# Adding three message parts in PSUM: 24 matmuls of 48 columns a batch in place of 8 of 144

## What is computed

```python
m = relu(node_feat[src] + edge_feat)
neigh = segment_sum(m, dst, num_segments=N)            # layer 1: one sum over edges
x = segment_sum(w[:, None] * x[c], r, num_segments=n)  # layer 2: this line twice
agg = segment_sum(x[src], dst, num_segments=n)         # layer 3: twice, with weights between
agg = segment_sum(adj_vals[:, None] * xw[edge_src], edge_dst, num_segments=N)  # layer 4
```

## Time and profile before

| | us |
|---|---|
| median of 3 runs (lowest, highest) | 10436.51 (10404.52, 10447.85) |
| the profiled execution | 10414.08 |
| its span | 10412.4 |
| six sum stages, from the first gather's record to the next pass's work | about 510 to 530 each |

### The profile page before, as it was taken

How to read it: one execution, slowest core, us unless ns; L and a number is a source line. 1 busy time by engine, 2 the same in 40 slices (tenths; PEclk the granted TensorE clock), 3 DMA queues, 4 the chain that set the end, 5 groups by cost and what they waited for, 6 DMA issues and landing times.

```text
span 10412.4 us, 220272 instructions
## 1 busy us (share of the span) xinstructions
PE 6955.9 (67%) x59989; PEld 5588.1 (54%) x59990; DVE 6952.4 (67%) x15309; ACT 3898.3 (37%) x9751; POOL 4440.2 (43%) x4277
## 2 busy tenths in 40 slices
PE   9999999997045557555675667456765576555676
PEld 9766666665034445444554455345554455555555
DVE  6544444443488887777667766777757776799874
ACT  0455555554167850066005610264016600344200
POOL 0477777777077227400770057102740076000373
PEclk9855555555555557577766766677667776555565
DMA  8233333333879877688776877688768878255675
GB/s 327 64 88 87 88 89 89 86 87 110 267 226 249 264 252 223 143 289 294 226 200 235 290 241 213 176 295 268 220 148 293 292 221 197 102 195 195 201 220 117
DMA packets 1037429, 2048.13 MB, mean 197 GB/s; under 512 B 354974, under 2 KB 476318, under 8 KB 1036958
## 3 DMA queue, kind: packets, MB, share of 16 engines
q1 hardware_dynamic: 764830, 1267.16, 37.8%
q0 software_dynamic: 242832, 700.42, 25.5%
q10 hardware_dynamic: 29680, 79.57, 2.0%
HBM read 1263.63 MB, written 783.00 MB: 197 GB/s over the span
## 4 chain that ended last, share of the span: by engine, by line
DMA 23%; POOL 21%; PE 18%; issue 17%; DVE 16%; DVEq 3%; ACT 1%; POOLq 0%; SPq 0%; ACTq 0%
POOL edge_rows L446 15%; DMA WORK<-messages_in_parts,source 13%; PE psum L778 6%; DVE WORK L1055 6%; POOL WORK L479 6%; PE psum L797 5%; DMA BIG<-edge_rows 5%; DMA WORK<-parts_by_slot 4%; PE psum L664 3%; DVE WORK L1093 2%; DVE BIG L1086 2%; ACT WORK L585 1%; DVEq L67 1%; PE psum L733 1%; PE psum L783 1%
## 5 line engine op out<-in xcount | busy, mean ns | idle before, releaser
L479 POOL DMA_INDIRECT WORK<-messages_in_parts,source x2220 | 2280.4, 1027 | 4544.1 <-DMA messages_in_parts<-WORK 3763.7
L797 PE MATMUL psum<-WORK 128*128 128x144 bf16 x17760 | 2219.8, 297 | 960.4 <-DMA WORK<-messages_in_parts,source 628.4
L797 PEld LDWEIGHTS psum<-WORK 128*128 128x128 bf16 x17760 | 1806.6, 158 | 1373.0 <-issue 674.8
L446 POOL DMA_INDIRECT edge_rows<-WORK x1664 | 1709.6, 1027 | 862.5 <-issue 857.9
L778 PE MATMUL psum<-BIG,WORK 128*128 x11840 | 1287.8, 277 | 1038.2 <-DVE WORK L1055 601.3
L585 ACT CAST WORK<-psum 128x432 bf16<-128x432 f32 x2960 | 1382.5, 522 | 1415.2 <-PE psum L778 1355.6
L862 DVE TENSOR_TENSOR WORK<-lane_k,slot_part 128x1024 bf16<-128x1024 bf16 x2220 | 1529.6, 690 | 481.9 <-PE psum L797 344.3
L1055 DVE TENSOR_SCALAR WORK<-WORK,here 128x1024 bf16<-128x1024 uint8 x2220 | 1667.8, 751 | 98.4 <-DMA WORK<-parts_by_slot 78.9
L778 PEld LDWEIGHTS psum<-BIG,WORK 128*128 128x128 bf16 x11840 | 1013.5, 121 | 1312.6 <-issue 1308.9
L783 PE MATMUL psum<-BIG,WORK 128*128 x17760 | 957.9, 215 | 839.6 <-DVE WORK L1055 732.9
L783 PEld LDWEIGHTS psum<-BIG,WORK 128*128 128x128 bf16 x17760 | 834.9, 116 | 962.7 <-issue 928.9
(11 more groups left out here) (175 smaller groups left out, 7326.7 us busy)
## 6 DMA issues: line engine op xcount, KB each, us to landing
messages_in_parts<-WORK SPq DMA_DIRECT2D x2220, 288.0 KB
WORK<-parts_by_slot SPq DMA_DIRECT2D x444, 640.0 KB, 4.9
BIG<-edge_rows SPq DMA_DIRECT2D x148, 1040.0 KB
WORK<-blocks_by_edge SPq DMA_DIRECT2D x416, 256.0 KB, 3.5
edge_rows<-BIG ACTq DMA_DIRECT2D x1, 76960.0 KB, 209.9
WORK<-in_edge_attr_dram SPq DMA_DIRECT2D x415, 96.0 KB, 2.2
WORK<-messages_in_parts,source POOLq DMA_INDIRECT x2220, 4.1
edge_rows<-WORK POOLq DMA_INDIRECT x1664
```

The lines of the kernel that those rows point to most:

```text
L446: pool.indirect_dma_start(rows_dram, bass.IndirectOffsetOnAxis(ap=at_stage[g][:, j:j + 1], axis=0), row_buf[g][:, j, :], None).then_inc(s_ ...
L479: pool.indirect_dma_start(msg[c].rearrange("p k f -> p (k f)"), None, unit_dram, bass.IndirectOffsetOnAxis(ap=source[d][:, t:t + 1], axis= ...
L797: m = pe.matmul(sum_bank(c), onehot[c % GB][:, :, k], msg[c][:, k, :], start=k == 0, stop=k == K - 1)
```

## The change

In the sum stage PE writes 48 columns for a batch instead of 144: for each k three matmuls with the same weights and one third of the message each, all 24 accumulated into the same columns. A batch has a PSUM bank of its own (five banks in turn), PE waits for `sums_added` of the batch five before instead of for the reduce of a pair, and DVE adds the 48 PSUM columns straight to the aggregate. `reduce_pair`, `pair_sum` and the semaphore `pair_sums_reduced` are gone.

```diff
@@ -204,7 +204,6 @@
         SEL = [carve(128, [T * K], BF16) for _ in range(GB)]
         part_row = [carve(128, [GB, T * K], U8) for _ in range(2)]
         msg = [carve(128, [K, W3], BF16) for _ in range(RING)]
-        pair_sum = [carve(P, [2, D]) for _ in range(GB)]
         select = [s.rearrange("p (k u) -> p k u", k=K) for s in SEL]
         onehot = [s.rearrange("p (m k) -> p m k", k=K) for s in SEL]
         z = [H[:, j * K * D:(j + 1) * K * D].rearrange("p (k f) -> p k f", f=D) for j in range(GB)]
@@ -251,8 +250,7 @@
                                            sem("degrees_summed"))
         s_store = [sem(f"messages_stored{c}") for c in range(RING)]
         s_gath = [sem(f"messages_gathered{c}") for c in range(RING)]
-        s_oh, s_sum, s_reduced, s_added = (sem("onehots_ready"), sem("batches_summed"), sem("pair_sums_reduced"),
-                                           sem("sums_added"))
+        s_oh, s_sum, s_added = sem("onehots_ready"), sem("batches_summed"), sem("sums_added")
         s_var, s_std = sem("variance_ready"), sem("deviation_ready")
         s_ones, s_node, s_tr, s_trc = (sem("bias_rows_ready"), sem("aggregate_ready"), sem("blocks_transposed"),
                                        sem("transposes_copied"))
@@ -277,7 +275,7 @@
 
         def sum_bank(c):
 
-            return bank[c // 2][:, c % 2 * W3:(c % 2 + 1) * W3]
+            return bank[c % GB][:, 0:D]
 
         def spread_bank(c, k):
 
@@ -791,10 +789,11 @@
                         n = i * RING + (c + q * BATCHES)
                         pe.wait_ge(s_gath[c], i * 16 + (q * PAIRS + 1) * 16)
                         pe.wait_ge(s_oh, n + 1)
-                        if c % 2 == 0:
-                            wait_past(pe, s_reduced, i * GB + (c // 2 + q * (BATCHES // 2) - (GB - 1)))
+                        wait_past(pe, s_added, n - (GB - 1))
                         for k in range(K):
-                            m = pe.matmul(sum_bank(c), onehot[c % GB][:, :, k], msg[c][:, k, :], start=k == 0, stop=k == K - 1)
+                            for f in range(3):
+                                m = pe.matmul(sum_bank(c), onehot[c % GB][:, :, k], msg[c][:, k, f * D:(f + 1) * D],
+                                              start=k == 0 and f == 0, stop=k == K - 1 and f == 2)
                         m.then_inc(s_sum, 1)
 
                 rounds(pe, PAIRS, sum_batches)
@@ -1110,21 +1109,13 @@
                             stage(PAIRS - 1, c)
                 dve.wait_ge(s_spread, (q + 1) * BATCHES)
 
-                def reduce_pair(i, c):
-
-                    m = i * GB + (c // 2 + q * (BATCHES // 2))
-                    dve.wait_ge(s_sum, i * RING + (c + 2 + q * BATCHES))
-                    wait_past(dve, s_added, i * RING + (c + 2 - RING + q * BATCHES))
-                    v.tensor_reduce(pair_sum[c // 2], bank[c // 2][:, 0:2 * W3]
-                                    .rearrange("p (a c f) -> p a f c", a=2, c=3), AX.X, ALU.add).then_inc(s_reduced, 1)
-
                 def add_sum(i, c, b):
 
                     n = i * RING + (c + q * BATCHES)
-                    dve.wait_ge(s_reduced, i * GB + (c // 2 + q * (BATCHES // 2) + 1))
+                    dve.wait_ge(s_sum, n + 1)
                     wait_past(dve, s_added, n)
                     o = AGG[:, ds(b * D, D)]
-                    v.tensor_tensor(o, o, pair_sum[c // 2][:, c % 2, :], ALU.add).then_inc(s_added, 1)
+                    v.tensor_tensor(o, o, sum_bank(c), ALU.add).then_inc(s_added, 1)
 
                 def collect(i):
 
@@ -1139,16 +1130,11 @@
                             add_sum(i, c - LAG, its_block[c])
                         elif not isinstance(i, int):
                             add_sum(i - 1, RING + c - LAG, its_block[c])
-                        if c % 2 == 1 and c > 1:
-                            reduce_pair(i, c - 3)
-                        elif c % 2 == 1 and not isinstance(i, int):
-                            reduce_pair(i - 1, RING - 2)
 
                 if q == 0:
                     dve.wait_ge(s_mcopied, 1)
                 rounds(dve, PAIRS, collect)
                 last = load_blocks(dve, batch_regs[0:LAG], batch_block[d][0:1, BATCHES - LAG:BATCHES])
-                reduce_pair(PAIRS - 1, RING - 2)
                 for k in range(LAG):
                     add_sum(PAIRS - 1, RING - LAG + k, last[k])
                 dve.wait_ge(s_added, (q + 1) * BATCHES)
```

## The result

| | before | changed |
|---|---|---|
| median (lowest, highest), us | 10420.51 (10403.05, 10447.85), 4 runs | 10534.44 (10514.31, 10561.96), 4 runs |
| the profiled execution, us | 10414.08 | 10514.31 |
| its span, us | 10412.4 | 10512.6 |

The ratio is 1.0109, with a 95% interval of 1.0069 to 1.0149: 1.1% slower, 114 us by the medians. The direction and the mechanism are those of the forecast; the forecast size, 268 us, was more than double.

What follows compares the result with a forecast made beforehand. POOL bounds the sum stages' first part at 1.344 us a batch; 24 loads of 64 ns make PE the bound at 1.536: +46 us a stage, +278 for six, less 10, so 10,705 us, range 10,470 to 10,910.

Steps and rivals of the forecast that it cites:

- POOL bounds the first four fifths, and DVE's saving is worth nothing: Sum stage, first part: POOL's gather and idle set 1.344 us a batch; DVE's 0.23 us reduce is saved without gain.
- The price is a strided weight load, three times as many: Sum-stage matmuls on PE: each loads weights 8 elements apart, 24 loads a batch instead of 8, 1.536 us a batch.
- The load's size, between 54 and 64 ns, taken as 64: Strided weight load on PE: bracketed from two groups of eight matmuls; at 64 ns, 24 make 1.536 us a batch.
- PE stays the bound: Last part of a sum stage: gathers need 1.68 us but run about 15 us ahead and fall back only 10 us.
- The ends of the stages, 10 us: From last reduce to next pass's work: 1.90 us falls to about 0.3, giving 1.6 us a pass, 10 in all.
- Half and full clock give the same: Sum-stage matmuls on PE: 1.536 us a batch at either clock level, since 48 columns need 40 ns even at 1.2 GHz.
- A: Sum-stage loads: strided loads are cheap when nothing separates them, POOL still bounds, 10,427 us, no change; chance 0.09.
- B: Sum-stage gathers on POOL get shorter, from 1.039 to 0.96 us, as compares come evenly: 10,284 us; chance 0.07.
- C: PE's stream of matmuls breaks at every batch, paying one load's 64 ns again, 1.60 us a batch: 10,847 us; chance 0.12.
- D: Half clock makes closely following strided loads dearer, 100 ns each, 2.4 us a batch: 12,620 us; chance 0.03.
- DVE's looser order: DVE's wait in the sum stage: adds run four batches behind, so PE has four compares ahead; counted as zero.
- The estimate of 59 ns: Strided weight load as four chunks of 32 columns at 1.84 ns a column: 59 ns, a sum of 10,440 us.

Runs made afterwards that it cites:

- the DVE part alone: Changed kernel with 8 matmuls of 144 columns, no reduce, DVE adding only the 48 high-part columns: 10441.81 us, ratio 1.0016 to the kernel before.
- the spread run: Changed kernel with each empty slot gathering a row of its own instead of row 0: 10499.07 us, ratio 1.0080 to the kernel before.
- the PE part alone: Kernel before with 24 matmuls of 48 columns a batch into separate thirds of 144 columns, reduce and adds kept: 10707.18 us, ratio 1.0271.

## Why the prediction was right or wrong, step by step

**POOL bounds the first four fifths, and DVE's saving is worth nothing.** Right: the DVE part alone changed nothing, and with weights 4 apart, where PE has room, the whole change costs no more than 0.4%.

**The price is a strided weight load, three times as many.** Right, and shown from two sides: half the columns left the 60 ns, and packed weights, with the same accumulation, took them away. That POOL's cadence comes back when the load is cheap is shown by the run with weights 4 apart.

**The load's size, between 54 and 64 ns, taken as 64: this is the step that failed.** It is 60.0 ns. The 64 ns between L797's loads belong to its matmuls. L778, with the same 144 columns and packed weights, has its matmuls almost as far apart at full clock, (0.67 - 0.23)/7 = 63 ns:

```profile
5702.52 0.67 PE L778 MATMUL psum<-BIG,WORK 128*128 x8 [0.35 <-ACT WORK L585]
```

So the spacing only bounded the load from above, and I took the bound for the value. The reason that I gave for the upper end fits the trace: in the group of the earlier trace rows each load from the third on starts 1 or 2 ns after the matmul ahead of it. But it says that the loads keep the matmuls' pace, and not how long a load needs. The 4 ns are 24 x 370 x 0.004 = 36 us a stage, 213 us in all. The range of the load was right; where in it the truth lay decided the size, since only the part above 56 ns costs anything: I forecast 8 ns above that point and it was 4.

**The last fifth, "PE stays the bound": wrong, a consequence of the same term and of the lead.** At 1.44 us a batch the 74 gathers fall back 74 x (1.68 - 1.44) = 18 us. The prediction counted a lead of about 15 us. In the trace of the changed kernel a gather starts 12 us before its batch's first matmul, and one took 4 us to land in the first part of the kernel before, so the lead was nearer 8 us, an estimate. With 64 ns and a fall of 10 us PE would have been at the edge of it; no run had that spacing. PE's timeline has its first wait for a gather 47 us into this part, and then one in every two to four batches:

```profile
5453.91 6.51 PE L795 MATMUL psum<-WORK 128*128 128x48 bf16 x96 [0.18 <-DMA WORK<-messages_in_parts,source]
```

From there on the transfers bound: 118 us for 74 batches. A stage became 543 us, not the 370 x 1.44 = 533 that PE alone needs; the spread run shows the 533. So the miss is -36 + 10 = -26 us a stage, -156 us in all: 268 - 156 = 112, for 114 measured by the medians.

**The ends of the stages, 10 us.** As forecast in the trace, 1.90 us down to 0.24.

**Half and full clock give the same.** For weights 8 apart only half clock is shown, 60.0 ns at 0.50; the granted clock was 0.50 in all six sum stages, so at full clock this stream never ran. Weights 4 apart cost 33 ns at both.

**The rivals of the prediction.** A (the load streams once nothing separates the loads) fell with the 60 ns in a stream of 5004. B (faster, through shorter gathers) fell with the unchanged gathers of both runs in which POOL bounds. C (breaks at each batch) fell with the same stream, and D (dearer at half clock) with its spacing. But C's idea was right for another cut of the change: the PE part alone does break, at every second turn of the loop, and I had counted DVE's looser order as zero. In the full change it is what keeps PE fed. This was a cost hidden by a cover that the change itself takes away, POOL's cadence, and the sum should have named it.

The Trainium skill's page "SBUF — State Buffer", section on the DMA port swizzle, has lines of 16 bytes with a penalty for each access to a new one; the runs agree with the penalty: 60 ns where each weight is in a line of its own, 33 where two share one, nothing measurable where four or eight do. The same note holds two accesses in a line to be enough for full bandwidth; here the measurement differs, 33 ns with two in a line against at most 25 with four.

The estimate of 59 ns that the prediction made from the four chunks of the Trainium skill's page "TensorE: Matmul & The Clock Gate" (weight-path perf modes) and L664's 1.84 ns a column was within 1 ns. That the load works in such chunks is not shown by this, since L664 also reads its moving operand 8 elements apart. The prediction's other reading of those words, that strided weights cost no more, did not hold: 60 ns against at most 26.

The time that the prediction set beside the 59 ns, 10,440 us, was 94 us too low although the load was right: one ns of spacing is 53 us, and the last fifth, where the transfers bound, adds six times 10.

## What to carry to other kernels

Splitting a matmul into narrower ones multiplied the weight loads here, also where the weights were the same; what counts then is the load, and that goes with the distance between weights in SBUF, so lay them out for PE before you split, in a way that still leaves two neighbours for the engine that writes them. Two costs of a change can hide each other: price each part for the bound that holds after the whole change, not for the one of today. And cut a stage by time as well as by engine: one fifth with another bound hid about 40% of this cost (114 us in place of 197), and was itself the best thing to mend.

## What the runs showed that was not expected

**The clock.** In the changed kernel PE never stops in the first four fifths of a sum stage, and the granted clock is 0.50 throughout (1.2 GHz); before, with PE idle for 29% of the time, it was 0.71 in the same stretch. In the run with packed weights PE pauses too, and the mean over this stretch is 0.77:

```profile
5100.00:5300.00 200.00, 131.45 (x3365) 115.24 (x3363) 176.19 (x281) 0.00 (x0) 145.23 (x140) 0.77 0.70 207
```

No run was made to find out why. The lower level costs the loads nothing as far as is shown: with weights 4 apart they take 33 ns at either, and in the kernel before the first load of a batch, weights 8 apart, lasts 142 ns at full clock and 143 at half.

**The compare.** 1024 bf16 elements take 0.69 us with 8, 4 or 2 neighbours of the repeated operand in the innermost loop and 1.217 us with one.

**Gathers of one row.** In the last fifth, gathers whose 128 units are all the same row of 2304 bytes came with 172 GB/s in all; with different rows it was 217.
